# A second query tile placed by 32x32 block transposes and DRAM instead of TensorE transposes

## What is computed

```python
xn  = layernorm(x)                                  # 1024 x 256
q, k, v = split(xn @ qkv_w + qkv_b)                 # 16 heads of 128
scores = q @ k.T + alibi(head)                      # causal, slope 2 ** (-head / 2), no 1/sqrt(d)
ctx = softmax(scores) @ v
attn = ctx @ out_w + out_b
gate, up = xn @ lut[gate_idx].T, xn @ lut[up_idx].T # 688 inner channels, weights from a table of 16
out = x + attn + (silu(gate) * up) @ lut[down_idx].T
```

## Time and profile before

| | |
|---|---|
| median of 3 runs | 517.88 us (517.37 to 518.29) |
| the profiled execution | 519.0 us |
| its span, first to last instruction | 517.2 us |
| mean granted TensorE clock | 0.996 |

### The profile page before, as it was taken

One profiled execution on the slowest core, in us unless ns is written; L12 is line 12 of the kernel. 1 busy time (PEld: TensorE's weight loads), 2 busy tenths in 40 slices (PEclk: granted clock), 3 DMA queues, 4 the chain that ended last, 5 costly groups with the idle time before them and its releaser, 6 DMA issues. The chain is left out here.

```text
span 517.2 us, 10365 instructions
## 1 busy us (share of the span) xinstructions
PE 506.4 (98%) x3142; PEld 455.1 (88%) x3142; DVE 414.9 (80%) x1044; ACT 320.1 (62%) x656; POOL 340.6 (66%) x372
## 2 busy tenths in 40 slices
PE   7998999999999999999999999999999998999997
PEld 6786989989899889988998989988998897998897
DVE  6698797889788988989798978898898978764451
ACT  4786665767575756576675756585657656664430
POOL 3446776688767965787578876796678567962300
PEclk9998999999999999999999999999999999999999
DMA  7942030203011110203020302021011101010001
GB/s 267 133 87 67 0 94 1 73 21 91 0 54 37 46 46 4 69 19 91 0 71 20 91 0 67 24 48 43 28 43 27 46 14 38 3 52 1 0 22 61
DMA packets 19846, 24.56 MB, mean 47 GB/s; under 512 B 2288, under 2 KB 13552, under 8 KB 19696
## 3 DMA queue, kind: packets, MB, share of 16 engines
q1 hardware_dynamic: 18784, 23.24, 14.7%
q0 software_dynamic: 1040, 1.05, 2.4%
HBM read 17.99 MB, written 6.29 MB: 47 GB/s over the span
## 5 line engine op out<-in xcount | busy, mean ns | idle before, releaser
L1111 POOL TENSOR_TENSOR w_ffn<-w_ffn,term 128x1088 f32<-128x1088 f32 x60 | 152.7, 2545 | 73.7 <-DVE term L934 73.7
L719 ACT ACTIVATE work<-work,neg_max 128x128 f32<-128x128 f32 (+7 forms) x128 | 98.8, 772 | 34.6 <-DVE neg_max L919 34.6
L919 DVE CUSTOM_DVE_ANT_0 work<-ps_s,alibi 128x128 f32<-128x128 f32 (+7 forms) x128 | 96.0, 751 | 5.4 <-issue 4.9
L947 DVE TENSOR_TENSOR p_t_lo<-ps_t,p_t_hi 128x512 fp32r<-128x512 f32 (+3 forms) x160 | 85.5, 559 | 15.6 <-ACT p_t_hi L726 15.5
L1089 POOL TENSOR_SCALAR work<-work,inv_sum 128x128 f32<-128x128 f32 (+7 forms) x128 | 95.8, 748 | 0.0
L726 ACT ACTIVATE p_t_hi<-ps_t 128x512 fp32r<-128x512 f32 (+3 forms) x160 | 74.1, 496 | 26.2 <-PE ps_t L570 26.1
L570 PE MATMUL ps_t<-ident,work 128*128 128x128 f32 x496 | 73.6, 275 | 1.7 <-DVE p_t_lo L947 1.6
L448 PE MATMUL ps_u<-p_t_hi,v_hi 128*128 128x512 f32 x192 | 66.5, 346 | 2.3 <-DVE p_t_lo L962 1.9
L702 ACT ACTIVATE qk_hi<-ps_u,bias_now 128x512 fp32r<-128x512 f32 x64 | 44.2, 691 | 37.9 <-PE ps_u L450 37.8
L448 PE MATMUL ps_s<-qk_hi 128*128 128x128 f32 (+2 forms) x192 | 67.2, 350 | 0.5 <-DVE qk_lo L895 0.5
L450 PE MATMUL ps_u<-p_t_hi,v_lo 128*128 128x512 f32 x192 | 66.9, 349 | 0.0
(11 more groups left out here) (123 smaller groups left out, 1187.3 us busy)
## 6 DMA issues: line engine op xcount, KB each, us to landing
scratch<-blocks SPq DMA_DIRECT2D x64, 80.0 KB, 2.3
raw<-scratch SPq DMA_DIRECT2D x16, 320.0 KB, 2.9
qk_raw<-w_qk SPq DMA_DIRECT2D x16, 256.0 KB, 2.8
w_ffn<-idx SPq DMA_DIRECT2D x1, 2176.0 KB, 10.7
v_raw<-w_v SPq DMA_DIRECT2D x8, 256.0 KB, 2.7
o_raw<-w_o SPq DMA_DIRECT2D x8, 256.0 KB, 3.0
acc<-b_out POOLq DMA_DIRECT2D x1, 1024.0 KB, 18.1
out<-acc SPq DMA_DIRECT2D x8, 128.0 KB, 1.7
```

What stands on the lines that cost most here:

```text
L719: act.activation(slot(i), slot(i), ACT.Exp, bias=neg_max[:, col:col + 1], scale=-1.0, accum_out=row_sum[:, col:col + 1]).then_inc(exp_done, 1)
L919: dve.tensor_tensor_reduce(slot(i).rearrange("p (b c) -> p b c", b=banks), made_of, alibi[:, p, S - width:S].rearrange("p (b c) -> p b c", ...
L947: dve.tensor_tensor(p_rows(1, i, g), ps_t[:, room, 0:len(turned(i, g)) * P].rearrange("p (j q) -> p j q", q=P), p_rows(0, i, g).bitcast(F3 ...
L1111: pool.tensor_tensor(piece, piece, term[:, :], ALU.add).then_inc(term_added, 1)
```

## The change

Tile 5 (the sixth) is treated as tile 4 is: `PLACED = 4, 5`. `raw`, `blocks`, the scratch and the semaphores for leaving and coming back are there for each of the two tiles. `turn` skips both. Both block transposes are in DVE's step 6, tile 4's first. SP issues the four stores of tile 4, those of tile 5, then the two loads back. ACT places tile 4 in step 1 and tile 5 in step 2, DVE both in step 2. `mask` of tile 0 and of tile 1 waits for a block transpose.

Besides, the steps of other work are dealt anew: `qk_lo` and its high part go from step 6 to 4, the output weights' split from 5 to 3, the sums from steps 1, 2, 4, 7 to 0, 2, 6, 7, the look-ups of the steady pairs from 1, 2, 4, 7 to 0, 2, 3, 7 (those of the first pair's second head stay), and units move between steps in all three tables. In the tail, turn 5 goes, placed 4 comes first and placed 5 behind turn 7.

```diff
-QK_W_AT = 6
+QK_W_AT = 4
 V_W_AT = 2
-O_W_AT = 5
+O_W_AT = 3
 ALIBI_AT = 3
-SUM_AT = 1, 2, 4, 7
+SUM_AT = 0, 2, 6, 7
 FFN_LO_AT = {3: 0, 4: 1, 6: 2, 7: 3}
 LAG = 3
-BLOCKS_AT = 6
-PLACED_HI_AT = 2
-PLACED_LO_AT = 2
+BLOCKS_AT = 6, 6
+PLACED_HI_AT = 1, 2
+PLACED_LO_AT = 2, 2
 
...
-PLACED = 4
-BAND = (PLACED + 1) * B32
-GROUPS = [-(-(i + 1) // 4) if i != PLACED else 0 for i in range(NT)]
+PLACED = 4, 5
+BLOCK_COLS = sum(i + 1 for i in PLACED) * P
+GROUPS = [-(-(i + 1) // 4) if i not in PLACED else 0 for i in range(NT)]
...
 UNITS = {
     FIRST: [
-        (("q1", -1), ("k1", 1), ("nq0", 2), ("v0", 3), ("v1", 4), ("nk0", 5), ("pv0", 7), ("v2", 7)),
-        (("v3", 0), ("q1", 1), ("k1", 2), ("_pv1-", 3), ("_pv1", 4), ("nk0", 5), ("nq0", 6),
+        (("q1", -1), ("k1", 0), ("nk0", 4), ("v0", 4), ("v1", 6), ("nq0", 6), ("v2", 7), ("pv0", 7)),
+        (("k1", 0), ("v3", 1), ("q1", 2), ("nq0", 3), ("_pv1-", 3), ("_pv1", 4), ("nk0", 5),
          ("pv0", 7)),
     ],
     STEADY: [
-        (("q1", 0), ("k1", 0), ("_out0", 1), ("_out1", 2), ("nq0", 3), ("_pv1-", 4), ("_pv1", 4),
-         ("nk0", 5), ("v0", 5), ("v1", 6), ("v2", 6), ("pv0", 7)),
-        (("k1", 0), ("q1", 0), ("_out2", 1), ("v3", 2), ("_out3", 2), ("_pv1-", 4), ("_pv1", 4),
+        (("q1", 0), ("_out0", 0), ("_out1", 0), ("k1", 1), ("nq0", 2), ("nk0", 3), ("_pv1-", 4),
+         ("_pv1", 4), ("v0", 5), ("v1", 6), ("v2", 6), ("pv0", 7)),
+        (("k1", 0), ("_out2", 0), ("q1", 1), ("v3", 2), ("_out3", 3), ("_pv1-", 4), ("_pv1", 4),
          ("nq0", 5), ("nk0", 6), ("pv0", 7)),
     ],
     LAST: [
-        (("k1", 0), ("_out0", 1), ("q1", 1), ("_out1", 2), ("nq0", 2), ("_pv1-", 4), ("_pv1", 4),
-         ("nk0", 5), ("v0", 5), ("v1", 6), ("v2", 7), ("pv0", 7)),
-        (("k1", 0), ("q1", 2), ("_out2", 3), ("v3", 4), ("_out3", 4), ("_pv1-", 5), ("_pv1", 6),
+        (("k1", 0), ("q1", 0), ("_out0", 0), ("_out1", 1), ("nk0", 2), ("nq0", 3), ("_pv1-", 4),
+         ("_pv1", 4), ("v0", 6), ("v1", 6), ("v2", 7), ("pv0", 7)),
+        (("_out2", 0), ("v3", 1), ("k1", 1), ("_out3", 2), ("q1", 3), ("_pv1-", 3), ("_pv1", 5),
          ("pv0", 7)),
     ],
 }
 
-TAIL = (("turn", 5), ("placed", PLACED), ("gate_up", 0), ("out", 0), ("out", 1), ("turn", 6), ("gate_up", 1), ("turn", 7),
-        ("gate_up", 2), ("pv", 1), ("gate_up", 3), ("out", 2), ("gate_up", 4), ("gate_up", 5),
+TAIL = (("placed", 4), ("gate_up", 0), ("out", 0), ("out", 1), ("turn", 6), ("gate_up", 1), ("turn", 7),
+        ("placed", 5), ("gate_up", 2), ("pv", 1), ("gate_up", 3), ("out", 2), ("gate_up", 4), ("gate_up", 5),
         ("out", 3), ("gate_up", 6), ("gate_up", 7), ("gate_up", 8), ("gate_up", 9), ("gate_up", 10),
...
-TERM_FIRST_AT = 2, 3, 6, 7
+TERM_FIRST_AT = 3, 4, 6, 7
 TERM_SECOND_AT = 1, 2, 4, 7
-TERM_AT = 1, 2, 4, 7
-TERM_LATE_AT = 0, 3, 4, 7
+TERM_AT = 0, 2, 3, 7
+TERM_LATE_AT = 0, 2, 3, 7
...
             def move(n, p):
 
-                sp.wait_ge(blocks_turned, head_no(n, p) + 1)
-                for a in range(BANDS):
-                    sp.dma_start(scratch[:, :, a, :].rearrange("b p x -> p b x"),
-                                 blocks[a * B32:(a + 1) * B32, :, :, :].rearrange("p b j c -> p b (j c)")
-                                 ).then_inc(blocks_out, 16)
-
-                sp.wait_ge(blocks_out, n * (32 * BANDS) + (p + 1) * (16 * BANDS))
-                sp.dma_start(raw[:, :], scratch[:, :, :, :].rearrange("b p a x -> (b p) (a x)")).then_inc(blocks_back, 16)
+                for t, i in enumerate(PLACED):
+                    sp.wait_ge(blocks_turned, n * (2 * len(PLACED)) + p * len(PLACED) + t + 1)
+                    for a in range(BANDS):
+                        sp.dma_start(scratch[t][:, :, a, :].rearrange("b p x -> p b x"),
+                                     blocks_of(i)[a * B32:(a + 1) * B32, :, :, :].rearrange("p b j c -> p b (j c)")
+                                     ).then_inc(blocks_out[t], 16)
+                for t, i in enumerate(PLACED):
+                    sp.wait_ge(blocks_out[t], n * (32 * BANDS) + (p + 1) * (16 * BANDS))
+                    sp.dma_start(raw[:, part_of(i)],
+                                 scratch[t][:, :, :, :].rearrange("b p a x -> (b p) (a x)")).then_inc(blocks_back[t], 16)
...
 
                     pe.wait_ge(p_lo, groups_to(n, p, 3 if c == 0 else -1))
                     if c == 1:
-                        pe.wait_ge(placed_lo, head_no(n, p))
+                        pe.wait_ge(placed_lo, head_no(n, p) * len(PLACED))
...
             def turn(n, p, i, back):
 
-                if i == PLACED:
+                if i in PLACED:
                     return
                 pe.wait_ge(normed, tile_no(n, p, i - NT if back else i) + 1)
...
-            def place_hi(n, p):
-
-                act.wait_ge(blocks_back, n * 32 + p * 16 + 16)
-                act.activation(placed_rows(0), placed_raw(), ACT.Copy).then_inc(placed_hi, 1)
+            def place_hi(n, p, t):
+
+                i = PLACED[t]
+                act.wait_ge(blocks_back[t], n * 32 + p * 16 + 16)
+                act.activation(placed_rows(0, i), placed_raw(i), ACT.Copy).then_inc(placed_hi, 1)
...
-                        if i == PLACED_HI_AT and not (kind == FIRST and p == 0):
-                            place_hi(n, p - 1)
+                        for t in range(len(PLACED)):
+                            if i == PLACED_HI_AT[t] and not (kind == FIRST and p == 0):
+                                place_hi(n, p - 1, t)
...
-                if i == 0 and not (kind == FIRST and p == 0):
-                    dve.wait_ge(blocks_turned, head_no(n, p))
+                if i < len(PLACED) and not (kind == FIRST and p == 0):
+                    dve.wait_ge(blocks_turned, (head_no(n, p) - 1) * len(PLACED) + i + 1)
                 elif i >= 4 or not (kind == FIRST and p == 0):
                     dve.wait_ge(p_turned, groups_to(n, p, i - 4))
...
-            def turn_blocks(n, p):
-
-                dve.wait_ge(normed, tile_no(n, p, PLACED) + 1)
+            def turn_blocks(n, p, t):
+
+                i = PLACED[t]
+                dve.wait_ge(normed, tile_no(n, p, i) + 1)
                 if not (isinstance(n, int) and n == 0 and p == 0):
-                    dve.wait_ge(blocks_out, n * (32 * BANDS) + p * (16 * BANDS))
-                dve.transpose(blocks[:, :, :, :].rearrange("p b j c -> p j b c"),
-                              slot(PLACED).rearrange("p (j b c) -> p j b c", b=BANDS, c=B32)).then_inc(blocks_turned, 1)
-
-            def place_lo(n, p):
-
-                dve.wait_ge(placed_hi, head_no(n, p) + 1)
-                dve.tensor_tensor(placed_rows(1), placed_raw(), placed_rows(0).bitcast(F32),
+                    dve.wait_ge(blocks_out[t], n * (32 * BANDS) + p * (16 * BANDS))
+                dve.transpose(blocks_of(i).rearrange("p b j c -> p j b c"),
+                              slot(i).rearrange("p (j b c) -> p j b c", b=BANDS, c=B32)).then_inc(blocks_turned, 1)
+
+            def place_lo(n, p, t):
+
+                i = PLACED[t]
+                dve.wait_ge(placed_hi, head_no(n, p) * len(PLACED) + t + 1)
+                dve.tensor_tensor(placed_rows(1, i), placed_raw(i), placed_rows(0, i).bitcast(F32),
                                   ALU.subtract).then_inc(placed_lo, 1)
...
-                        if i == PLACED_LO_AT and not (kind == FIRST and p == 0):
-                            place_lo(n, p - 1)
-                        if i == BLOCKS_AT:
-                            turn_blocks(n, p)
+                        for t in range(len(PLACED)):
+                            if i == PLACED_LO_AT[t] and not (kind == FIRST and p == 0):
+                                place_lo(n, p - 1, t)
+                        for t in range(len(PLACED)):
+                            if i == BLOCKS_AT[t]:
+                                turn_blocks(n, p, t)
```

More of the change, by code:

```diff
@@ L195, in block_ffn @@
         work = sb("work", [P, sum(SLOT_W)])
-        raw = sb("raw", [P, BANDS * BAND])
-        blocks = sb("blocks", [P, BANDS, PLACED + 1, B32])
+        raw = sb("raw", [P, BLOCK_COLS])
+        blocks = sb("blocks", [P, BLOCK_COLS])
         xn_t = [sb(f"xn_t_{s}", [P, KT, S], F32R) for s in ("hi", "lo")]
@@ L249, in block_ffn @@
         unit_used, term_ready = sem("unit_used"), sem("term_ready")
-        blocks_turned, blocks_out = sem("blocks_turned"), sem("blocks_out")
-        blocks_back = sem("blocks_back")
+        blocks_turned = sem("blocks_turned")
+        blocks_out, blocks_back = [[sem(f"blocks_{i}_{where}") for i in PLACED] for where in ("out", "back")]
         placed_hi, placed_lo = sem("placed_hi"), sem("placed_lo")
@@ L258, in block_ffn @@
         qk_w_lo, v_w_lo, o_w_lo, ffn_w_lo = sem("qk_w_lo"), sem("v_w_lo"), sem("o_w_lo"), sem("ffn_w_lo")
-        scratch = nc.dram_tensor("scratch", (BANDS, B32, BANDS, BAND), F32).ap()
+        scratch = [nc.dram_tensor(f"scratch_{i}", (BANDS, B32, BANDS, (i + 1) * B32), F32).ap() for i in PLACED]
```

(16 more changed lines are left out.)

## The result

The change made the kernel slower by 0.7%: 521.61 us median of 4 runs (520.19 to 522.95) against 518.09 for the kernel before beside it (4 runs), ratio 1.0069 [1.0039, 1.01]. The forecast of 509.8 and its range up to 516.0 are both missed. The profiled execution took 520.19 us, span 518.4, against 519.0 and 517.2.

The account below looks back on a forecast made before the run. TensorE's work was taken as the bound. The terms -9.9 + 0.9 + 0.7 + 0.2 gave -8.1 us: 510.9 us for the profiled execution, 509.8 for the median, range 505.5 to 516.

Parts of the forecast that it names:

- Step 1: Tile 5's six transposes per head leave TensorE: 0.62 us per head, 9.9 us gained in all.
- Busy for all of it: TensorE was read as busy throughout a steady pair of heads, 55.72 us, before the change.
- Step 2: DVE's load per head: both place_lo run alone, 0.81 and 0.97 us, without port collision; 48.3 us per pair.
- The agreement "to 0.01 us": Claim that profile rows match the rule of DVE and GpSimd shutting each other out, to 0.01 us.
- Step 3: Gates where TensorE waits for DVE: no `_pv1-` stall; out0 of even heads short by 0.25, half booked, 0.9 us.
- Step 4: Other moved instructions: look-ups, qk_w_lo from step 6 to 4 with SP's refill, loads back; cost 0.
- Step 4 again: Moved look-ups: step 0's sum clears place_lo; step 3's look-up waits about 1 us for a sum, hidden.
- Step 5: First and last pair: second head's stall 2.7 us instead of 1.95, +0.7; half clock there about 1.7 us; last pair +0.2.
- Partly given back: Rival, chance 0.18: TensorE stalls 0.3 to 0.5 us in each of 15 heads, time 513 to 516.
- The port decides: Rival, chance 0.08: POOL's sum and norm still collide with both place_lo, 19 us of stalls, time 529.

Follow-up runs that it names:

- e11_one: Changed kernel with only the fifth tile placed, the sixth again through TensorE, all else as newly dealt: 525.42 us, ratio 1.0133.
- e9_odd: On experiment 5's kernel, the odd heads' step 0 look-up moved behind tile 6's low part in step 1, its sum behind norm 0: 510.18 us, ratio 0.9837.
- experiment 4: Changed kernel with both tiles placed but the old steps for all other work, only the tail as changed: 538.41 us, ratio 1.0368.
- Experiments 1 and 5: 1: changed kernel, first head's q/k split in step 6: 522.41 us. 5: also second head's look-ups like steady heads', SP moving blocks ahead of refill: 513.88 us.
- e2_term: Changed kernel with the first pair's second head looking up in steps 0, 2, 3, 7 instead of 1, 2, 4, 7: 517.91 us, ratio 0.9989.
- e6_order: Changed kernel with the odd heads' step 0 look-up between the low parts of the step's two units: 523.97 us, ratio 1.0119.

## Why the prediction was wrong

- **Step 1, the transposes:** right in size. Between e11_one and after, which share the deal, a pair differs by 1.25 us once the waits named above and e11_one's 0.30 ahead of out0 and 0.27 ahead of out1 are taken off; 1.24 was expected. The pair of e9_odd is 1.16 us shorter than before, but two things cancel in that number. It still has out0's wait, and the kernel before lost some 0.4 us per pair in step 4: from turn 1 to `_pv1-` it took 0.20 and 0.31 us, start to start, where after takes 0.14 and 0.13, and turn 1 itself came some 0.1 us late. "Busy for all of it" hid this, because the rows of matmuls overlap.
- **Step 2, DVE and the port:** right. 640 and 768 columns take 1.68 us together on their own (expected 1.7 with overlap), DVE has 47.96 us per pair (48.3), and experiment 4 shows the collision that the new deal avoids, 2.60. The agreement "to 0.01 us" is not in the rows: place_lo ends 0.68 us after the sum, and alone it takes 0.81.
- **Step 3, the gates:** neither `_pv1-` stalls in the steady pairs. out0 waits 0.32 us for an expected 0.25; I booked half of it, and it comes in full: 7 x 0.32 = 2.2 us instead of 0.9.
- **Step 4, "qk_w_lo moves from step 6 to 4 ... cost 0": the step that failed.** The move was priced in a steady pair, with its refill landed long ago and for SP and POOL alone. Its reader on ACT was not followed into the first head. There it made the first head 6.5 us longer where 0.6 less was expected: 7.1 us of the 9.3 that separate the profiled execution from its sum (520.2 against 510.9). Experiments 1 and 5 show the chain by undoing it, and experiment 11 shows that the second block transpose, which the prediction priced in steady heads only, has 0.9 us of PE's wait.
- **Step 4 again, the look-up in step 0 of the odd heads.** I asked what the sum meets and what the look-up of step 3 waits for, and found both (DVE waits 1.2 us for the sum, hidden). I did not ask what the look-up of step 0 meets. It meets norm 7 and is longer by 0.7 us, ahead of the low part that frees turn 7's room. 0.62 us in each of 7 odd heads, 4.3 us; e9_odd is 3.7 us faster without it. Over heads 3 to 15 the kernel came out 2.7 us worse than the sum: 1.3 from out0, 3.7 from the six odd heads among them, less 2.3, about half of it in the steady pairs (the short waits of step 1) and half in the 15th head, which had waits of its own before.
- **Step 5, the first pair:** the mechanism was right (the sum ahead of norm 0), the wait 3.10 us instead of 2.7, and no half clock behind it. Where before had 0.57 from 49 to 53 us, after has 1.00, so that head came out 0.6 us better than the sum. One row of a table takes the wait away (e2_term), for 1.3 us in that head.
- **The rivals.** "Partly given back" is what the steady pairs did, at 0.32 and 0.62 us per head for the 0.3 to 0.5 it named. It left out that a move is made in the first head too, and its 516 was the end of the range. "The port decides" did not come in after, where both place_lo run alone in the steady pairs.

## What to carry to other kernels

When an instruction that reads a refilled buffer is moved earlier, find the landing of its first refill in the trace of the first iteration, and then list what is queued behind the reader on its own engine: a steady iteration cannot show this. When a bound engine is relieved, waits that its own work just covered come out, as the one ahead of turn 7 did, so compare all its gates with the new arrival time, the small rooms of buffers too, and ask of each moved instruction what runs beside it in its new place. A DMA queue's order is part of the same question: here one exchange of two lines on SP was worth 4 us.

## What was not expected of the hardware

- A DVE instruction with one uint8 input in SBUF (the look-up) is also drawn out by a POOL instruction: 1.55 us beside norm 7 of 1.12, and 1.67 in e6_order, against 0.83 alone. In both cases it starts just behind the norm and ends 0.6 us after the norm's end, as place_lo ended 0.68 us after the sum's. The Trainium skill (SBUF — State Buffer, "Who interferes with whom") names tensor_scalar among the operations that can take the port pair shared with GpSimd; the trace agrees, and the prediction had drawn on its rule for two SBUF inputs only.
- The length of a stall did not tell whether the clock fell. Behind 3.67 us it was 0.50 for 6 us, behind 3.81 in e2_term 0.72 over the same stretch, behind 3.10 at 53.8 us and behind 2.39 in e11_one there was none, behind 1.95 before there was 0.57 for 4 us. What that last one costs is seen in the runs of the kernel before: with a mean clock of 1.0 it took 517.31 us, at 0.997 most often 519.0, the 1.7 us of step 5. What decides whether the clock falls behind a wait is not shown here.
